# Window attention: heads of a band gathered and projected once per own row, value projection moved ahead

## The chip, the cores and the metric

One Trainium2 chip, one core. The program is one launch; the metric is the device time of the launch in microseconds. TensorE does the matrix products, VectorE and GpSimd elementwise work and small transposes, ScalarE exponentials and copies, SyncE issues the DMA transfers. TensorE's clock has two levels, 1.2 and 2.4 GHz; the profile tells the granted share of the upper one.

## What is computed

The part that the change touches is attention over overlapping windows, cut from the reference (the softmax and the sums are shortened here):

```python
def _L0_conv_ref(x, norm1_w, norm1_b, wq, wk, wv, wproj, ...):      # x (2, 96, 256, 256)
    tops = _positions(h, step, ps); lefts = _positions(w, step, ps)  # ps 16, step 14: 19 x 19 windows
    crop = x[:, :, row_idx[:, None, :, None], col_idx[None, :, None, :]]
    tok = crop.transpose(0, 2, 3, 4, 5, 1).reshape(b * n, ps * ps, c)
    y = _layernorm(tok, norm1_w, norm1_b)
    q, k, v = heads(y @ wq), heads(y @ wk), heads(y @ wv)            # 4 heads, 16 / 16 / 24 wide
    attn = softmax(q k^T / sqrt(16)); out = attn v
    tok = out @ wproj + tok
    acc = zeros_like(x).at[windows].add(tok)
    x2 = acc * fh * fw                  # rows and columns that two windows share count one half each
    ... MLP with a depthwise 5 x 5 convolution on x2, then a clustering block ...
```

Before it, the whole network input is brought to zero mean and unit variance by groups of three channels, which the kernel folds into a scale and a shift for each channel and image (`gn_scale`, `out_shift`, the latter with the projection's constant part).

## The kernel before

The function `attention` walks over 38 bands (19 per image, two images), each a strip of 16 rows by 256 columns, and over the 19 windows of a band, each 16 by 16 = 256 tokens. Band tops and window lefts are 14 apart, the last only 2 after the one before (238, 240). So neighbours share 2 rows or columns, the last two share 14. `own_rows` is the number of rows of a band that no later band touches: 14, for the last but one 2, for the last 16.

All engines run the same loop over windows n = 0 .. 721, written out by hand as a software pipeline. Each engine takes its instructions in the order of the code and waits on counting semaphores. In iteration n TensorE issues:

- `scores_for_max(n, 0)` (line 677): bf16 products of keys and queries for two heads, whose maxima VectorE takes (line 753)
- in windows 5 to 12 of a band, `queries_and_keys` (line 662): one chunk, 512 token columns, of the next band's queries and keys. ScalarE copies it to `packed` (line 613) and SyncE spreads it over the partitions of `q` and `k` in eight transfers for two chunks (line 480)
- `scores(n - 1)` (line 689): 16 records of fp32 products against the queries less maxima (`qaug`, line 777)
- `projection(n - 5)` (line 712): one fp32 product of 256 columns out of `ot`; ScalarE copies it to `prs` (line 632) and GpSimd adds it into `acc` (line 572)
- `scores_for_max(n, 1)`, the other two heads
- `attended(n - 2)` (line 700): the value products, exponentials times values with a column of ones for the denominators
- `values(n - 1)` (line 707): the value projection of a window; ScalarE copies it into `vaug` (line 619)
- `maxima(n)` (line 719): the maxima transposed

VectorE in iteration n: `maxima(n, 0)`, `turn(n - 3)` (line 760, value products to tokens on partitions), `maxima(n, 1)`, `denominators(n - 3)` (line 764), `turn_back(n - 4)` (line 770, a transpose of 256 elements per partition in blocks of 32) and `queries_less_maxima(n)` (line 777). ScalarE: the chunk's copy, `exponential(n - 1, 0)`, `projected(n - 5)`, `exponential(n - 1, 1)` (line 626), `values(n - 1)`. The bank `lin_ps` is shared by the chunk, the projection and the value projection: `lin_free` makes TensorE wait until ScalarE has copied the last one out.

GpSimd: `normalise` (lines 555, 559) multiplies a window by reciprocals and by the half shares; `add`; `turn_columns` (line 542) turns one eighth of the next band's rows to token order, in windows 2 to 9; `scale` (line 549) prepares `acc` as x times scale plus shift; `both` (line 583) adds x once more for the second output. What a band leaves to the next is copied from one `acc` buffer to the other (line 576).

SyncE per band, in this order: load x into `xr` (line 504), spread pair 0, store x2 (line 509), spread pairs 1 and 2, store xs (line 515), load x into `acc` (line 470), spread pair 3, load y (line 466), four transfers that unroll convolution taps (line 490, 768 pieces of 256 bytes each). The x, y and store transfers have one contiguous run of 14336 or 16384 bytes per channel.

## Time and profile before

| | |
|---|---|
| median of three runs | 7228.42 us (7219.73 to 7231.93) |
| span of the profiled execution | 7234.2 us |
| attention stage in it | first window's maxima at 684.7 us, last at 4078.1 us |
| TensorE busy in the whole span | 6229.6 us (86%) |
| VectorE, ScalarE, GpSimd busy | 4977.8, 3555.8, 2561.1 us |

A matrix product is recorded with its drain, so one record overlaps the next and the distance from start to start is what TensorE spends. A fp32 product stands as two records. A timeline row groups instructions of one line that follow each other; what stands in brackets at its end is the idle time of the engine before it and what ended it. The trace's times are microseconds from the start of the span.

### The profile page before, as it was taken

What the parts mean: (1) busy time and instruction counts of PE and PEld (TensorE: products, weight loads), DVE (VectorE), ACT (ScalarE), POOL (GpSimd) and SP (SyncE); (2) the same over time, 40 slices, a digit from 0 to 9 for tenths busy, and PEclk for the clock granted to TensorE, in tenths of its full rate; (3) what the DMA queues carried; (4) which work ended last, traced back from release to release, by engine and by line L of the source; (5) the groups of instructions that cost most, each with busy time, mean ns of one, the idle gap of its engine ahead of it and who ended that gap; (6) DMA issues with size and microseconds to landing.
All of it is one profiled execution on the core that took longest, in us unless ns stands there. A gap on an engine that the chain in (4) does not pass through costs nothing. (4 is left out here: it accounts for less than half of the span.)

```text
span 7234.2 us, 138671 instructions
## 1 busy us (share of the span) xinstructions
PE 6229.6 (86%) x52604; PEld 3161.5 (44%) x52604; DVE 4977.8 (69%) x7538; ACT 3555.8 (49%) x5600; POOL 2561.1 (35%) x3401
## 2 busy tenths in 40 slices
PE   0885999999999999999999689979999566588885
PEld 0332555555554544555555333335555011076662
DVE  6785777777777777777777555548888445556664
ACT  0553666666666666666666356654444111143340
POOL 0443555555555555555555466630000000000000
PEclk9997999999999999999999899999999788789985
DMA  7785454554554444444544378879897999736666
GB/s 304 194 244 152 90 115 113 113 113 112 113 113 92 110 111 112 113 112 114 116 112 103 86 235 237 238 247 355 342 346 279 284 306 311 226 95 191 185 190 180
DMA packets 461711, 1303.16 MB, mean 180 GB/s; under 512 B 158148, under 2 KB 163268, under 8 KB 416964
## 3 DMA queue, kind: packets, MB, share of 16 engines
q1 hardware_dynamic: 400564, 1141.10, 56.2%
q10 hardware_dynamic: 53328, 102.85, 4.8%
q0 software_dynamic: 7168, 50.34, 2.0%
q8 instruction: 432, 7.08, 0.4%
q14 instruction: 219, 1.79, 0.1%
HBM read 731.14 MB, written 508.40 MB: 171 GB/s over the span
## 5 line engine op out<-in xcount | busy, mean ns | idle before, releaser
L753 DVE TENSOR_REDUCE at_mz<-at_ps 128x4 bf16<-128x1024 f32 x1444 | 1774.5, 1229 | 792.1 <-PE at_ps L677 791.5
L626 ACT ACTIVATE at_E<-at_ps 128x1024 f32<-128x1024 f32 x1444 | 1500.7, 1040 | 801.7 <-PE at_ps L689 801.7
L689 PE MATMUL at_ps<-at_qaug,at_k 32*128 32x256 f32 x11552 | 835.2, 403 | 79.2 <-DVE at_qaug L777 78.0
L700 PE MATMUL at_ps<-at_E,at_vaug 128*32 128x256 f32 x11552 | 776.9, 386 | 1.9 <-issue 1.9
L1216 PE MATMUL cv_ps<-cv_yin,cv_band 128*128 128x384 f32 x2304 | 746.0, 486 | 27.5 <-DMA cv_yin<-y_mlp 27.5
L1236 DVE TENSOR_TENSOR cv_yin<-cv_gl,cv_yin 64x384 f32<-64x384 f32 x1152 | 637.5, 553 | 151.3 <-ACT cv_gl L1227 143.5
L689 PEld LDWEIGHTS at_ps<-at_qaug,at_k 32*128 32x128 f32 x11552 | 525.4, 185 | 443.9 <-issue 226.0
L555 POOL TENSOR_TENSOR at_share<-at_rden,t_share 128x8 f32<-128x8 f32 x722 | 146.9, 204 | 1444.7 <-DVE at_rden L764 1444.6
L677 PE MATMUL at_ps<-at_k,at_q 32*128 32x256 bf16 x5776 | 580.7, 277 | 9.5 <-DMA at_k<-at_packed 7.4
L1216 PEld LDWEIGHTS cv_ps<-cv_yin,cv_band 128*128 128x128 f32 x2304 | 436.4, 189 | 337.4 <-DMA cv_yin<-y_mlp 28.4
L1227 ACT ACTIVATE cv_gl<-cv_ps,cv_bias 128x384 f32<-128x384 f32 x576 | 334.4, 581 | 438.4 <-PE cv_ps L1216 438.4
L1498 POOL MEMSET cs_eps<- 96x1 f32 x1 | 0.1, 95 | 1500.9 <-POOLq L1246 1500.9
L707 PEld LDWEIGHTS at_ps<-t_wv,at_y 96*128 96x128 f32 x2888 | 378.0, 190 | 301.2 <-issue 301.2
L707 PE MATMUL at_ps<-t_wv,at_y 96*128 96x96 f32 x2888 | 496.7, 295 | 2.5 <-issue 2.4
L572 POOL TENSOR_TENSOR at_acc<-at_prs,at_acc 96x256 f32<-96x256 f32 x722 | 495.1, 686 | 3.1 <-ACT at_prs L632 3.1
L712 PE MATMUL at_ps<-at_ot,t_wproj_heads 128*96 128x256 f32 x1444 | 487.4, 419 | 2.2 <-ACT at_prs L632 1.8
L559 POOL TENSOR_TENSOR at_on<-at_turned,at_share 128x256 f32<-128x256 f32 x722 | 444.1, 615 | 104.4 <-DVE at_ot L770 1.3
L1754 PE MATMUL cl_ps<-c_rhs,cl_xu 97*128 97x208 f32 x2048 | 445.4, 375 | 40.1 <-DMA cl_xu<-x 33.6
L1364 DVE SCALAR_TENSOR_TENSOR f_xa<-f_ps,f_b,f_xa 128x256 f32<-128x256 f32 x384 | 227.0, 667 | 345.7 <-PE f_ps L1347 344.9
L1754 PEld LDWEIGHTS cl_ps<-c_rhs,cl_xu 97*128 97x128 f32 x2048 | 395.1, 210 | 109.8 <-issue 67.3
L1344 PE MATMUL f_ps<-f_sa,f_wa 128*32 128x512 f32 (+1 forms) x1728 | 236.3, 619 | 239.9 <-DMA f_sbb<-s_mlp 238.3
L632 ACT ACTIVATE at_prs<-at_ps 96x256 f32<-96x256 f32 x722 | 426.9, 591 | 3.9 <-PE at_ps L712 3.6
(210 smaller groups left out, 9384.4 us busy)
## 6 DMA issues: line engine op xcount, KB each, us to landing
cv_yin<-y_mlp SPq DMA_DIRECT2D x48, 2340.0 KB, 14.7
s_mlp<-cv_yin SPq DMA_DIRECT2D x48, 2340.0 KB, 8.3
at_rows_in<-y_attention SPq DMA_DIRECT2D x38, 1536.0 KB, 14.4
gn_xin<-in_x SPq DMA_DIRECT2D x16, 3072.0 KB, 23.2
ln_xin<-in_x SPq DMA_DIRECT2D x192, 256.0 KB, 7.6
y_attention<-ln_xin SPq DMA_DIRECT2D x192, 256.0 KB, 3.8
cl_xu<-x SPq DMA_DIRECT2D x128, 384.0 KB, 3.8
cl_xv<-x SPq DMA_DIRECT2D x64, 768.0 KB, 6.4
```

Source lines behind the costliest of these rows:

```text
L559: pool.tensor_tensor(on[:, s, :].rearrange("p (a d) -> p a d", d=VC), turned[:, s, :].rearrange("p (a d) -> p a d", d=VC), share[:, s, :]. ...
L572: pool.tensor_tensor(a, prs[:, m % 2, :].rearrange("p (r c) -> p r c", c=PS), a, ALU.add).then_inc(added, 1)
L626: act.activation(E[:, m % 2, 2 * p:2 * p + 2, :], psum[:, 2 + 2 * p:4 + 2 * p, :], ACT.Exp).then_inc(exp_done, 1)
L677: i = pe.matmul(psum[:, g, TOK * j:TOK * j + TOK], q_upper[rows, n % 2, tokens(w, 128 * j, 128)], k_upper[rows, n % 2, tokens(w)], start=T ...
L689: i = pe.matmul(psum[:, 2 + h, TOK * j:TOK * j + TOK], k[rows, n % 2, tokens(w, 128 * j, 128)], qaug[rows, m % 2, :], start=True, stop=True)
L700: i = pe.matmul(pv_ps[32 * h:32 * h + VC, 0:TOK], vaug[:, m % 2, z, h, :], E[:, m % 2, h, z * TOK:(z + 1) * TOK], start=(z == 0), stop=(z ...
L707: i = pe.matmul(lin_ps[:, j * C:(j + 1) * C], y[0:C, n % 2, tokens(w, 128 * j, 128)], t["wv"][:], start=True, stop=True)
L712: pe.matmul(lin_ps[0:C, 0:TOK], t["wproj_heads"][:], ot[:, m % 2, :], start=True, stop=True).then_inc(proj_done, 1)
L753: dve.tensor_reduce(mz[:, m % 2].rearrange("p j (h c) -> p h j c", c=32)[:, 2 * p:2 * p + 2, :, DQ], psum[:, 0:2, :].rearrange("p h (j n) ...
L1216: m = pe.matmul(psum[:, n % NB, 0:3 * RUN], band[:, s, c, a, :], yin[:, s, c, 3 * u:3 * u + 3, GAP * a:GAP * a + RUN], start=(a == 0), sto ...
L1236: i = dve.tensor_tensor(yc, gl[half_rows(f), n % NG, :].rearrange("p (t n) -> p t n", n=RUN), yc, ALU.add)
L1754: m = pe.matmul(psum[:, 2 * half + g // 2, 256 * (g % 2):256 * (g % 2) + NFC], xu[:, n % XS, 128 * tile:128 * tile + 128], t["rhs"][:, f * ...
```

## The change

For each window, `normalise` no longer writes a buffer of its own but weighs the turned heads into `heads`, a buffer of 128 column pairs for the whole band. The pair that two windows share is weighted, waited for and added (four GpSimd instructions in place of two). When a group of 16 pairs is complete, after windows 2, 4, 6, 9, 11, 13, 15 and 18 (`WHOLE_AT`), `turn_back` transposes it in one instruction of 512 elements per partition into `ot`, a band buffer with 32 columns x 16 rows per chunk. `save` keeps the rows that the next band shares before they are overwritten, `join` adds them. The projection runs once for each own row, as eight products of 32 columns x own rows (448, 64 or 512 columns), in windows 0 to 7 of the next band; ScalarE copies it with the shift as bias into `xa`, and GpSimd adds x times scale (`residual`, two instructions per chunk, windows 1 to 8) and then x once more (`both`, windows 9 to 16). There is no `acc` and no `prs`, and x is loaded once.

The queries-and-keys chunks move from windows 5 to 12 to windows 8 to 15. `values(n - 1)` stands before `attended(n - 2)` on TensorE, and its copy between the two exponentials on ScalarE. y is loaded, x loaded and xs stored by half rows (128 columns, pieces of 512 bytes); `rows_in` holds half a band and is turned in windows 0 to 3 and 9 to 12. The loop runs eight iterations past the last window in place of five.

The diff, cut to its core:

```diff
+    CC = W // YP
+    PAIRS = W // 2
+    WHOLE_AT = (2, 4, 6, 9, 11, 13, 15, 18)
+    QK_AT = 8
+    END = NW + YP
...
-        rows_in = sb("rows_in", [C, PS * W])
+        rows_in = sb("rows_in", [C, PS, W // 2])
         y = sb("y", [C + 1, 2, W * PS])
-        acc = sb("acc", [C, 2, PS * W])
-        xr = sb("xr", [C, PS * W])
+        heads = sb("heads", [128, PAIRS, VC])
+        ot = sb("ot", [128, W, PS])
+        saved = sb("saved", [128, CC, STEP])
+        xscaled = sb("xscaled", [C, PS, CC])
+        xr = sb("xr", [C, PS, W])
+        xa = sb("xa", [C, PS, W])
...
+        def qk_at(n):
...
+            return (nb + 1, w - QK_AT) if n < NW and nb + 1 < NB and QK_AT <= w < QK_AT + YP else None
+
+        def whole(n):
+
+            nb, w = where(n)
+            return (nb, WHOLE_AT.index(w)) if 0 <= n < NW and w in WHOLE_AT else None
+
+        def proj_at(n):
+
+            nb, w = where(n)
+            return (nb - 1, w) if 1 <= nb <= NB and w < YP else None
...
+            def store_x2(n):
+                rows = own_rows(n)
+                sp.wait_ge(x2_done, YP * (n + 1))
+                sp.dma_start(rows_of(x2, n, 0, rows).rearrange("c r w -> c (r w)"), xa[:, 0:rows, :].rearrange("c r w -> c (r w)")).then_inc(x2_stored, 16)
+
+            def store_xs(n, half):
+                rows = own_rows(n)
+                sp.wait_ge(xs_done, YP * n + YP // 2 * (half + 1))
+                sp.dma_start(half_rows(xs, n, half, rows), xr[:, 0:rows, W // 2 * half:W // 2 * (half + 1)]).then_inc(xs_stored[half], 16)
...
+                more = n + 1 < NB
+                if more:
+                    load_y(n + 1, 1)
+                if n:
+                    store_x2(n - 1)
+                if more:
                     spread_heads(n + 1, 0)
-                if n >= 1:
-                    sp.wait_ge(added, NWIN * n)
-                    sp.dma_start(rows_of(x2, n - 1, 0, rows), acc[:, (n - 1) % 2, 0:rows * W]).then_inc(stored, 16)
-                if n + 1 < NB:
                     spread_heads(n + 1, 1)
+                if n:
+                    store_xs(n - 1, 0)
+                if n + 2 < NB:
+                    load_y(n + 2, 0)
+                if more:
                     spread_heads(n + 1, 2)
-                if n >= 1:
-                    sp.wait_ge(summed, sums(n - 1))
-                    sp.dma_start(rows_of(xs, n - 1, 0, rows), xr[:, 0:rows * W]).then_inc(xs_stored, 16)
-                    sp.wait_ge(stored, 16 * n)
-                    if n + 1 < NB:
-                        if carries(n):
-                            sp.wait_ge(carried, carries(n))
-                        load_x(n + 1)
-                if n + 1 < NB:
+                if n and n < NB:
+                    load_x(n, 0)
+                if more:
                     spread_heads(n + 1, 3)
-                if n + 2 < NB:
-                    load_y(n + 2)
-                if n >= 1:
+                if n:
+                    store_xs(n - 1, 1)
+                    if n < NB:
+                        load_x(n, 1)
                     unroll_taps((n - 1) * PER_BAND, PER_BAND)
...
-                pool.tensor_tensor(on[:, s, :].rearrange("p (a d) -> p a d", d=VC), turned[:, s, :].rearrange("p (a d) -> p a d", d=VC),
-                                   share[:, s, :].unsqueeze(2).to_broadcast([128, 8, VC]), ALU.mult).then_inc(on_done, 1)
-
-            def add(m):
-                n, w = where(m)
-                pool.wait_ge(pr_out, m + 1)
+
+                def shares(a, b):
+                    return share[:, s, a:b].unsqueeze(2).to_broadcast([128, b - a, VC])
+
                 if w == 0:
-                    pool.wait_ge(scaled, pieces(n))
-                    if carries(n):
-                        pool.wait_ge(carried, carries(n))
-                if m:
-                    pool.wait_ge(added, m)
-                a = window(acc, n % 2, w)
-                pool.tensor_tensor(a, prs[:, m % 2, :].rearrange("p (r c) -> p r c", c=PS), a, ALU.add).then_inc(added, 1)
-                if w == NWIN - 1 and n % NWIN < NWIN - 1:
-                    first = STEP if n % NWIN < NWIN - 2 else 2
-                    pool.wait_ge(added, m + 1)
-                    pool.tensor_copy(acc[:, (n + 1) % 2, 0:(PS - first) * W], acc[:, n % 2, first * W:]).then_inc(carried, 1)
-
-            def both(n, piece):
-                if piece == 0:
-                    pool.wait_ge(added, NWIN * (n + 1))
-                    pool.wait_ge(xr_loaded, 16 * (n + 1))
-                rows = slice(piece * 2 * W, (piece + 1) * 2 * W)
-                pool.tensor_tensor(xr[:, rows], xr[:, rows], acc[:, n % 2, rows], ALU.add).then_inc(summed, 1)
+                    pool.tensor_tensor(heads[:, 0:8, :], turned[:, s], shares(0, 8), ALU.mult).then_inc(heads_done, 1)
+                elif w < NWIN - 1:
+                    pool.tensor_scalar(turned[:, s, 0, :], turned[:, s, 0, :], share[:, s, 0:1], None, ALU.mult).then_inc(weighted, 1)
+                    pool.tensor_tensor(heads[:, first + 1:first + 8, :], turned[:, s, 1:8, :], shares(1, 8), ALU.mult)
+                    pool.wait_ge(heads_done, m)
+                    pool.wait_ge(weighted, weightings(m))
+                    pool.tensor_tensor(heads[:, first, :], heads[:, first, :], turned[:, s, 0, :], ALU.add).then_inc(heads_done, 1)
...
+            def save(n, c):
+                rows = shared_rows(n)
+                if rows:
+                    if n % NWIN == 1:
+                        pool.wait_ge(ot_done, YP * (n - 1) + c + 1)
+                    else:
+                        pool.wait_ge(joined, joins(n - 1, c))
+                    if joins(n, c) > 1:
+                        pool.wait_ge(joined, joins(n, c) - 1)
+                    pool.tensor_copy(saved[:, :, 0:rows], ot[:, cols(c), PS - rows:PS]).then_inc(saved_done, 1)
+
+            def join(n, c):
+                rows = shared_rows(n)
+                if rows:
+                    pool.wait_ge(ot_done, YP * n + c + 1)
+                    pool.wait_ge(saved_done, joins(n, c))
+                    a = ot[:, cols(c), 0:rows]
+                    pool.tensor_tensor(a, a, saved[:, :, 0:rows], ALU.add).then_inc(joined, 1)
+
+            def residual(n, c):
+                rows = own_rows(n)
+                if c % 4 == 0:
+                    pool.wait_ge(x_loaded[c // 4], 16 * (n + 1))
+                if YP * n + c:
+                    pool.wait_ge(x2_done, YP * n + c)
+                pool.tensor_scalar(xscaled[:, 0:rows, :], xr[:, 0:rows, cols(c)], t["gn_scale"][:, n // NWIN:n // NWIN + 1], None, ALU.mult).then_inc(scaled, 1)
+                pool.wait_ge(pr_out, YP * n + c + 1)
+                pool.wait_ge(scaled, YP * n + c + 1)
+                a = xa[:, 0:rows, cols(c)]
+                pool.tensor_tensor(a, a, xscaled[:, 0:rows, :], ALU.add).then_inc(x2_done, 1)
+
+            def both(n, c):
...
+            for n in range(END + 1):
+                nb, w = where(n)
+                if whole(n - 5):
+                    join(*whole(n - 5))
                 if 0 <= n - 3 < NW:
                     normalise(n - 3)
-                if n >= 5:
-                    add(n - 5)
-                nb, w = where(n)
-                if nb + 1 < NB and 2 <= w < 2 + YP:
-                    turn_columns(nb + 1, w - 2)
-                if 1 <= nb < NB:
-                    for piece in fresh(nb)[2 * w:2 * w + 2]:
-                        scale(nb, piece)
-                    if 5 <= w < 5 + own_rows(nb - 1) // 2:
-                        both(nb - 1, w - 5)
-            for piece in range(own_rows(NB - 1) // 2):
-                both(NB - 1, piece)
+                if whole(n - 3):
+                    save(*whole(n - 3))
+                if nb + 1 < NB and w < 4:
+                    turn_columns(nb + 1, w)
+                if nb + 1 < NB and 9 <= w < 13:
+                    turn_columns(nb + 1, w - 5)
+                if nb >= 1 and 1 <= w < 1 + YP:
+                    residual(nb - 1, w - 1)
+                if nb >= 1 and nb < NB and 9 <= w < 9 + YP:
+                    both(nb - 1, w - 9)
...
+            def projected(n, c):
+                rows = own_rows(n)
+                act.wait_ge(proj_done, YP * n + c + 1)
+                if c == 0 and n:
+                    act.wait_ge(x2_stored, 16 * n)
+                    act.wait_ge(xs_done, YP * n)
+                act.activation(xa[:, 0:rows, cols(c)].rearrange("p r c -> p c r"), lin_ps[0:C, 0:CC * rows].rearrange("p (c r) -> p c r", r=rows),
+                               ACT.Identity, bias=t["out_shift"][:, n // NWIN:n // NWIN + 1]).then_inc(pr_out, 1)
...
+                if qk_at(n):
+                    queries_and_keys(*qk_at(n))
+                if proj_at(n):
+                    projected(*proj_at(n))
                 if 0 <= n - 1 < NW:
                     exponential(n - 1, 0)
-                if n >= 5:
-                    projected(n - 5)
-                if 0 <= n - 1 < NW:
+                    values(n - 1)
                     exponential(n - 1, 1)
...
+            def projection(n, c):
+                rows = own_rows(n)
+                if shared_rows(n):
+                    pe.wait_ge(joined, joins(n, c))
+                else:
+                    pe.wait_ge(ot_done, YP * n + c + 1)
+                pe.matmul(lin_ps[0:C, 0:CC * rows], t["wproj_heads"][:], ot[:, cols(c), 0:rows], start=True, stop=True).then_inc(proj_done, 1)
...
+            chunks, projected = YP, 0
+            for n in range(END):
                 if n < NW:
                     scores_for_max(n, 0)
-                if chunk_at(n):
-                    lin_free(n - 1, 0, n - 5)
-                    queries_and_keys(*chunk_at(n))
+                if qk_at(n):
+                    lin_free(n - 1, chunks, 0)
+                    queries_and_keys(*qk_at(n))
                     chunks += 1
+                if proj_at(n):
+                    lin_free(min(n - 1, NW), chunks, projected)
+                    projection(*proj_at(n))
+                    projected += 1
                 if 0 <= n - 1 < NW:
                     scores(n - 1)
-                if n >= 5:
-                    lin_free(min(n - 1, NW), chunks, n - 5)
-                    projection(n - 5)
                 if n < NW:
                     scores_for_max(n, 1)
+                if 0 <= n - 1 < NW:
+                    lin_free(n - 1, chunks, projected)
+                    values(n - 1)
                 if 0 <= n - 2 < NW:
                     attended(n - 2)
...
+            def turn_back(n, c):
+                dve.wait_ge(heads_done, NWIN * n + WHOLE_AT[c] + 1)
+                if shared_rows(n):
+                    dve.wait_ge(saved_done, joins(n, c))
+                if n:
+                    dve.wait_ge(proj_done, YP * (n - 1) + c + 1)
+                dve.transpose(ot[:, cols(c), :].rearrange("p c r -> p (c r)"),
+                              heads[:, 16 * c:16 * c + 16, :].rearrange("p a d -> p (a d)")).then_inc(ot_done, 1)
```

## Rows read from the trace of the kernel before

**Rows 1.** Busy time by stretch (busy us and count per engine, PEclk, DMA share, GB/s)
```profile
2500.00:2600.00 100.00, 97.97 (x1040) 50.42 (x1033) 75.58 (x129) 63.23 (x95) 57.73 (x90) 1.00 0.51 113
```

**Rows 2.** Waits in 1500 to 3500 us (total, times, longest us)
```profile
PE at_ps L689 <- DVE at_qaug L777: 44.9, 243, 0.2
```

**Rows 3.** All instructions of line 753 (duration ns min/median/max, first and last start)
```profile
L753 DVE TENSOR_REDUCE at_mz<-at_ps x1444: 1223/1230/1232, 684.7 to 4078.1; 128x4 bf16<-128x1024 f32 x181
```

**Rows 4.** Timeline of TensorE, two windows (start us, us, then the instruction)
```profile
2531.95 0.40 PE L677 MATMUL at_ps<-at_k,at_q 32*128 32x256 bf16 x4
2532.32 1.12 PE L662 MATMUL at_ps<-at_y,t_wqk 97*128 97x512 f32 x2
2533.38 1.15 PE L689 MATMUL at_ps<-at_qaug,at_k 32*128 32x256 f32 x16
...
2537.12 0.40 PE L677 MATMUL at_ps<-at_k,at_q 32*128 32x256 bf16 x4
2537.70 1.15 PE L689 MATMUL at_ps<-at_qaug,at_k 32*128 32x256 f32 x16 [0.18 <-DVE at_qaug L777]
2538.78 0.67 PE L712 MATMUL at_ps<-at_ot,t_wproj_heads 128*96 128x256 f32 x2
2539.39 0.40 PE L677 MATMUL at_ps<-at_k,at_q 32*128 32x256 bf16 x4
2539.72 1.07 PE L700 MATMUL at_ps<-at_E,at_vaug 128*32 128x256 f32 x16
...
2541.24 0.28 PE L719 MATMUL at_ps<-t_neg_eye,at_mz 128*128 128x128 bf16 x2
2541.45 0.40 PE L677 MATMUL at_ps<-at_k,at_q 32*128 32x256 bf16 x4
```

**Rows 5.** Timeline of VectorE in the second of these windows
```profile
2539.83 1.23 DVE L753 TENSOR_REDUCE at_mz<-at_ps 128x4 bf16<-128x1024 f32 x1 [0.69 <-PE at_ps L677]
...
2541.08 0.40 DVE L770 STREAM_TRANSPOSE at_ot<-at_on 128x256 f32<-128x256 f32 x1
2541.55 0.42 DVE L777 TENSOR_TENSOR at_qaug<-at_ps,at_q 128x256 f32<-128x256 f32 x1
```

**Rows 6.** Timeline of ScalarE in both windows
```profile
2533.49 0.60 ACT L613 ACTIVATE at_packed<-at_ps 128x512 f32<-128x512 f32 x1 [1.22 <-PE at_ps L662]
...
2538.92 1.02 ACT L626 ACTIVATE at_E<-at_ps 128x1024 f32<-128x1024 f32 x1 [1.48 <-PE at_ps L689]
2539.84 0.59 ACT L632 ACTIVATE at_prs<-at_ps 96x256 f32<-96x256 f32 x1
2540.22 1.05 ACT L626 ACTIVATE at_E<-at_ps 128x1024 f32<-128x1024 f32 x1
```

**Rows 7.** Groups by line in 1500 to 3500 us, GpSimd (xcount | busy us, mean ns | idle)
```profile
L542 POOL COPY at_y<-at_rows_in 96x512 f32<-96x512 f32 x181 | 192.2, 1062 | 0.0
L583 POOL TENSOR_TENSOR at_xr<-at_xr,at_acc 96x512 f32<-96x512 f32 x151 | 191.3, 1267 | 0.0
...
L549 POOL TENSOR_SCALAR at_acc<-at_acc,t_gn_scale,t_out_shift 96x512 f32<-96x512 f32 x154 | 116.8, 766 | 0.0
```

**Rows 8.** Timeline of SyncE, DMA issues (start us, us until the last is issued)
```profile
2535.46 5.84 SPq L480 DMA_DIRECT2D at_q<-at_packed  x4
2541.35 2.50 SPq L480 DMA_DIRECT2D at_k<-at_packed  x4
...
2544.51 14.25 SPq L490 DMA_DIRECT2D tap_blocks<-tap_lines  x4
```

**Rows 9.** Line 480 in 2541.3 to 2543.8 us, and its landings
```profile
L480 SPq DMA_DIRECT2D at_k<-at_packed x4: 589/594/599, 2541.3 to 2543.3; - x4
...
DMA to landing us min/median/max: 8.8/9.0/10.4
```

**Rows 10.** Timeline of GpSimd at the end of the attention stage
```profile
4091.12 9.79 POOL L583 TENSOR_TENSOR at_xr<-at_xr,at_acc 96x512 f32<-96x512 f32 x8
4108.47 0.10 POOL L987 MEMSET f_eps<- 128x1 f32 x1 [7.56 <-POOLq L378]
```

153 lines of the change are left out of this document (66 added, 87 removed).

## The prediction

> **What bounds the kernel now.** I read the table of stretches first. In 100 us in the middle of the attention stage TensorE is busy 98%, VectorE 76%, ScalarE 63%, GpSimd 58%, and the granted clock is 1.00, the upper of its two levels [rows 1]. In the list of waits TensorE's own products have one entry: the score products wait for VectorE's queries less maxima, 44.9 us in 2000 [rows 2]. So TensorE's order sets the time, and its timeline prices a window. A window in which no queries and keys are projected goes, start to start from 2537.12 [rows 4]: first maxima product 0.58, of which 0.33 is work, as in the second, and 0.25 the wait for VectorE; scores 1.08; projection 0.61; second maxima product 0.33, value products and value projection together 1.52; transposed maxima (L719) 0.21. Sum 4.33 us. A window with a queries-and-keys chunk has 0.37 + 1.06 in place of the 0.58 and takes 5.17 (2531.95 to 2537.12). There are 37 x 8 = 296 of these and 426 of the others: 1530 + 1845 = 3375 us. The maxima run from 684.7 to 4078.1 [rows 3], 721 windows and some 2 us, or 3391 us: the two prices hold to 0.5%.
>
> From the second maxima product to L719 TensorE has 0.33 + 1.52 = 1.85 of work. VectorE needs as much: its reduction starts 0.44 after the product (2539.39 to 2539.83) and takes 1.23 [rows 4, 5], and 0.18 later, at 2541.24, L719 starts, its weight load included. A tie: a shorter TensorE order gains nothing there.
>
> **The change part by part.** Count from the first maxima product of a window as 0.
>
> Projection out of each window. Removed: 722 products of 256 columns, 0.61 each. The clean window keeps its 0.58 up to the scores (the L719, L777, scores path is untouched), then 1.08, so TensorE could start the second maxima product at 1.66. It must wait for the first reduction: 0.44 + 1.23 and some 0.06 for the hand-over, 1.73 (an estimate: the 0.18 above less the load of 128 columns). Then 1.85 and 0.21: **3.80**, 0.53 less than 4.33.
>
> Windows with a chunk. 0.33 + 1.06 + 1.08 + 1.85 + 0.21 = **4.53**, 0.64 less than 5.17; the 0.04 beside the 0.61 is the wait before L662 on the value copy, which now comes between the exponentials.
>
> Projection per own row. 37 bands are projected inside the loop, in the eight windows 0 to 7, which have no chunk. 34 of them have 14 rows, 448 columns. Between 0.61 for 256 and 1.06 for 512 that is 0.61 + 0.75 x 0.45 = 0.95: window 0.33 + 0.95 + 1.08 + 1.85 + 0.21 = **4.42**, 0.09 more than 4.33. One band has 16 rows (4.53, 0.20 more) and two have 2 rows, whose 64 columns fit in the 0.25 wait (3.81, 0.52 less). 130 windows are left clean. The projection adds waits in front of all of TensorE's work: for a chunk's join and for the value copy of the window before. The last chunk of a band is turned back in window 3 of the next, joined in 4 and projected in 7; the value copy is done by 3.8. Free.
>
> Sum: 296 x 0.64 = 189, minus 272 x 0.09 = 24, minus 8 x 0.20 = 2, plus 16 x 0.52 = 8, plus 130 x 0.53 = 69: 240 us.
>
> VectorE's turn back. 722 transposes of 256 elements (0.40, [rows 5]) become 304 of 512. No row has that size; bounds 0.40 and 0.80. I take 0.69, with the slope of the reduction (1.23 for 1024). It stands in front of the queries less maxima, which started 0.07 after the transpose ended (2541.48 to 2541.55), so these come 0.13 later (nothing to 0.35 at the bounds). Where the scores start at 1.39 or 1.28 that is hidden. Two of the eight turns of a band (after windows 15 and 17) are followed by a clean window: 37 x 2 x 0.13 = 10 us, 26 at most.
>
> ScalarE. 722 copies of 0.59 go, 304 of 448 elements come. The old one (L632, 256 elements, stepped write) takes 0.59, the contiguous copy of 512 (L613) 0.60 [rows 6]. Bounds 0.55 and 0.59 x 448/256 = 1.03. L613 starts 1.17 after its product of 512 columns (2532.32 to 2533.49, [rows 4, 6]); this one 1.05 after, at 1.38, and ends by 2.41. The first exponential wants ScalarE at 1.28 + 1.21 = 2.49 (scores to exponential 1.21: 2537.70 to 2538.92 [rows 4, 6]) and the value projection wants the bank at 2.69, so even the upper end is free. The value copy between the exponentials: its product starts at 2.06 in a clean window and is ready some 0.7 later, its four short products done; the first exponential, started at 1.79, frees the engine at 2.71 (0.92 from start to start, [rows 6]). Some 0.05 of wait, and the second exponential (1.05) then ends near 4.1, 0.3 into the next window, whose scores start at 0.58. Free, with 0.3 us of cover; beyond it the scores wait.
>
> GpSimd. Normalise becomes four instructions with some more elements than now, bounded by one scaling (0.77) and by two turning copies (2.12); I take the middle, 1.45. A residual of a chunk is a scaling (0.77 for 512, so 0.69 for 448) and an add (1.27, so 1.13), with some 0.15 between them 1.97; turning a chunk 1.06; adding x once more 1.13 [rows 7]; save or join of 64 elements 0.3. Windows 1 to 3 hold normalise, turn, residual and a save or join, up to 4.8 us in 4.42: a backlog of 1 us. The following windows hold 3.4 to 3.8 and work it off. VectorE's turn back waits for it, with normalise one window before: about 3 us of cover. Nothing on the path. SyncE's store of x2 waits for the last residual, in window 8, and the first spreads stand behind it: issued at 7.4 to 12.4 after window 8 began and landed by 17, before ScalarE wants their buffer in window 12, at 19.6.
>
> SyncE and its queue. x is loaded once, not twice. But loads of y and x and stores of xs now go in halves of a row, 512-byte pieces, 1344 or 1536 to a transfer. The last whole xs store (1536 KB) goes out at 4100.91, where the adds end, and the next stage begins at 4108.47 [rows 10], 7.5 us; a half takes 3.7 to 7.5, I take 5. What is moved is the deadline: the last chunk of queries and keys is copied in window 15, not 12. With window 8 as 0, the copy ends at 33.8 (7 x 4.53 + 2.1) and the next band's first product comes at 8 x 4.53 + 3 x 3.80 = 47.6: 13.8 us for eight transfers. They need 5.0 us to issue (2.50 for four, [rows 8]). Now, behind a store and a load of 1344 KB, four took 5.84 to issue and the last four 8.8 to 10.4 to land [rows 8, 9]: from the copy's end at 2534.1 [rows 6] to the last landing at 2543.3 + 10.4 = 2553.7, 19.6 us. In the changed order the half store goes out at about 25.5 (the add of window 12), then half of y, then eight spreads (5), then at about 33 the half load that stands in front of the last spreads. Their bounds are 5 us with nothing in front and 19.6 with all of today's; with half of the load and no store I take 10 (halfway is 12), landing at 44 to 46. Cost 0, with 2 to 4 us of cover.
>
> [...]
>
> The end. The residual of the last band now comes after its last window. GpSimd then has three normalises (4.5), a save (1), two joins of 448 (2.2), eight residuals of 16 rows (17.6, with 0.77 + 1.27 + wait) and eight adds (10.2), 35.5 us starting some 5 us after the last window began, then a half store of 5: 45. Now it is 33: the last reduction, at 4078.1 [rows 3], starts 0.58 + 1.08 + 0.61 + 0.44 after its window, so that began at 4075.4, and the next stage begins at 4108.47 [rows 10]. Cost 12 us (8 to 18). The start I take as even: half of y is loaded and turned, then the other half, against less traffic before the first spreads (5 either way).
>
> **Sum.** 240 - 10 - 12 = 218 us. The profiled execution spans 7234.2, 0.08% above the median of 7228.4: 7234.2 - 218 = 7016, or 7011 against the median.
>
> **Rivals.**
> (a) The spreads come late. Landing 19.6 us after the copy, as now, would make every band start wait 19.6 - 13.8 = 5.8 us, 37 times 215: 7226. If the half transfers hold SyncE as the small pieces did (14.25 us for 3072 pieces, so 6.2 for 1344 and 7.1 for 1536), store, y load, eight spreads and x load take 6.2 + 7.1 + 5 + 6.2 from 25.5, so the last spreads begin at 50.0 and land at 57.5, 9.9 us late: 366 us, **7377**, slower than before. It decides from 13.8 us; 2 us beyond it cost 74 us (7085). For it: the same queue already shows the 19.6 and the 14.25. Against: the 14.25 came behind 1.5 MB of y and unlanded spreads, and half as much stands in front now.
> (b) ScalarE's stepped write. The new copy writes with a step of 1 KB, the old with 64 bytes. If it took twice the upper bound, 2.06, it would end at 3.44 and hold the value projection 0.75 us in 280 windows: 210 us, 7220. The rows speak against it: the exponential behind the old copy starts 0.38 after it (2539.84 to 2540.22, [rows 6]), so the extra is at its end, not in its rate.
> The Trainium skill (SBUF — State Buffer, Door 1) says that each access that crosses into a new 16-byte line pays a penalty. Both steps do so at every element, so by that rule the new copy costs no more per element than the old one.
> (c) GpSimd behind. If its instructions take 30% more than I price, windows 1 to 3 hold 6.2 us and 4 and 5 some 4.8: 5.4 + 0.8 of backlog when the turn back of window 6 wants its heads, 3 more than the cover: 3 x 37 = 110 us, 7120. With 10% more it is hidden. For it: no row has these short instructions; against: the large ones are priced from their own rows [rows 7].
> (d) More gain. If the 1.85 of the tie was TensorE's and shrinks in the new order, up to 0.05 x 722 = 36: 6975.
>
> **How the numbers follow.** Forecast 0.62 (6975 to 7050, which takes in the bounds of the transpose, the end and the start); (a) 0.19, of which 0.06 ends slower than before and the rest lies between 7050 and 7200; (b) 0.05; (c) 0.08; (d) below 6975 0.04; several small losses that together leave nothing, 0.02. Range **6970 to 7130**: below it 0.03, above it 0.15. A measurement of this kernel tells 0.2% from no change (14 us). Faster 0.87, same 0.04, slower 0.09. Likeliest time 7011.
>
> **What would show it.** Periods of 4.53, 4.42 and 3.80 between first maxima products; in clean windows VectorE idle only before the second reduction, and TensorE waiting for the first one as well as for the queries less maxima. TensorE busy near 96%. No wait of the first maxima product of a band for a transfer into q or k; if there is one, (a). The stepped copy under 1.1 us; if over 1.3, (b). GpSimd with idle time in windows 5 to 18; without, (c). A gap of about 45 us between the last window's start and the next stage. I would be wrong if the tie of 1.85 grew, since each 0.1 there is 72 us.

## The result: 1.7% faster, half of what was forecast

The changed kernel takes 7106.27 us (median of 4 runs, 7094.13 to 7128.61), the kernel before 7226.08 (4 runs, 7219.73 to 7231.93). The ratio is 0.9832, 95% interval 0.9810 to 0.9854: 120 us, or 1.7%, where 215 were forecast. The profiled execution spans 7126.8 us, against 7234.2. It is the slowest of the four, some 20 us above their median, so what is read from its trace lies at the upper end.

The profile after, first by stretch: the middle of the attention stage, and all but its end (busy us and count per engine, then the granted clock of TensorE, DMA share, GB/s).

```profile
2500.00:2600.00 100.00, 98.14 (x1078) 51.92 (x1074) 78.04 (x123) 65.20 (x87) 79.14 (x143) 1.00 0.43 96
685.00:3820.00 3135.00, 3068.36 (x32906) 1616.80 (x32908) 2395.30 (x3740) 1963.60 (x2646) 2302.01 (x4360) 0.97 0.46 97
```

In the 100 us that answer to [rows 1] all is as forecast: TensorE 98%, the clock at its upper level, GpSimd up from 58% to 79%. Over the whole stage the clock is 0.97. Two levels, 1 and 0.5, average to 0.97 when 6% of the time is at the lower one, 1.2 GHz: about 190 us of 3135. The same row of the kernel before has 0.99. (Over the stage up to its last reduction the clock's own records add up to 205 us at the lower level, and 42 in the kernel before.)

Windows of TensorE (start us, us): one with a projection, from 2404.12, and one that is clean, from 2479.53. One with a chunk stands further down, counted from product to product of L720 (2360.70 to 2365.22).

```profile
2404.12 0.40 PE L735 MATMUL at_ps<-at_k,at_q 32*128 32x256 bf16 x4
2404.45 0.99 PE L774 MATMUL at_ps<-at_ot,t_wproj_heads 128*96 128x448 f32 x2
2405.38 1.15 PE L747 MATMUL at_ps<-at_qaug,at_k 32*128 32x256 f32 x16
2406.36 0.39 PE L735 MATMUL at_ps<-at_k,at_q 32*128 32x256 bf16 x4
...
2408.51 0.40 PE L735 MATMUL at_ps<-at_k,at_q 32*128 32x256 bf16 x4
...
2479.53 0.40 PE L735 MATMUL at_ps<-at_k,at_q 32*128 32x256 bf16 x4
2480.11 1.15 PE L747 MATMUL at_ps<-at_qaug,at_k 32*128 32x256 f32 x16 [0.18 <-DVE at_qaug L843]
2481.26 0.40 PE L735 MATMUL at_ps<-at_k,at_q 32*128 32x256 bf16 x4
2481.59 0.69 PE L765 MATMUL at_ps<-t_wv,at_y 96*128 96x96 f32 x4
2482.20 1.07 PE L758 MATMUL at_ps<-at_E,at_vaug 128*32 128x256 f32 x16
2483.21 0.29 PE L781 MATMUL at_ps<-t_neg_eye,at_mz 128*128 128x128 bf16 x2
2483.43 0.40 PE L735 MATMUL at_ps<-at_k,at_q 32*128 32x256 bf16 x4
```

With a chunk, with a projection and clean they take 4.52, 4.39 (2404.12 to 2408.51) and 3.90 us, where 4.53, 4.42 and 3.80 were forecast and the kernel before had 5.17, 4.33 and 4.33 [rows 4]. At these prices a band would take 8 x 4.39 + 8 x 4.52 + 3 x 3.90 = 83.0 us, exactly the forecast 8 x 4.42 + 8 x 4.53 + 3 x 3.80. Yet a band takes 86.4 us in the mean and 84.3 in the median, first reduction to first reduction, and the mean of windows 12, 13, 14 and 15 of a band is 5.89, 5.56, 5.26 and 4.70 us, single ones up to 8.3. These four hold 21.4 - 18.1 = 3.3 us a band too much: 37 x 3.3 = 122 us.

What stands there, in the list of waits of 1500 to 3500 us (total, times, longest), some 23 bands:

```profile
ACT at_packed L670 <- DMA at_k<-at_packed: 71.1, 23, 5.0
PE at_ps L765 <- issue: 29.2, 23, 3.2
```

The first entry is new: in 23 of these 24 bands ScalarE's copy of a chunk waited for transfers that empty its buffer. In the worst of them (SyncE, TensorE and ScalarE by time, then two stretches around it):

```profile
2358.38 0.32 SPq L497 DMA_DIRECT2D x<-at_xa  x1
2358.80 6.92 SPq L512 DMA_DIRECT2D at_q<-at_packed  x4
2360.70 1.12 PE L720 MATMUL at_ps<-at_y,t_wqk 97*128 97x512 f32 x2
2365.22 1.13 PE L720 MATMUL at_ps<-at_y,t_wqk 97*128 97x512 f32 x2
2365.76 2.50 SPq L512 DMA_DIRECT2D at_k<-at_packed  x4
2370.15 0.60 ACT L670 ACTIVATE at_packed<-at_ps 128x512 f32<-128x512 f32 x1 [5.02 <-DMA at_k<-at_packed]
2370.85 0.66 PE L765 MATMUL at_ps<-t_wv,at_y 96*128 96x96 f32 x4 [3.20 <-issue]
```
```profile
2366.00:2371.00 5.00, 1.80 (x22) 1.10 (x22) 2.25 (x4) 0.85 (x2) 4.76 (x10) 1.00 0.61 103
...
2376.00:2382.00 6.00, 6.00 (x47) 3.04 (x43) 2.39 (x5) 2.53 (x4) 2.30 (x5) 0.50 0.96 224
```

The product of the chunk was ready, but the copy (L670) started 4.93 us after it began, not 1.17. The value projection needs the bank that this copy empties and stood still for 3.20 us. TensorE was busy 1.80 of 5 us, and then the granted clock went from 1.00 to 0.50, 2.4 to 1.2 GHz: two windows of 8.3 us. What it waited for is the first eight spreads (L512), which came behind the store of x2 (L497), which came behind the last residual.

Over the whole stage the wait comes in 35 of 36 bands and delays the copy by 0.7 to 2.8 us, by 3.8 in this one. The clock fell after it in 13 of them, for 3.4 to 27.3 us each. The four executions of the changed kernel, 7128.6, 7116.3, 7096.2 and 7094.1 us, had mean granted clocks of 0.928, 0.931, 0.933 and 0.935: the longer, the lower. The band without the wait is the one whose store has 2 rows, 192 KB:

```profile
2268.91 0.32 SPq L497 DMA_DIRECT2D x<-at_xa  x1
2269.34 2.42 SPq L512 DMA_DIRECT2D at_q<-at_packed  x4
```

Its residuals have 64 columns, so the store goes out 6.6 us after window 8 begins and not 9.9, and the four spreads behind it take 2.42 us to issue, not 6 to 7. They land at 14.9.

### The profile page after: what moved, and what is told of

The parts are those of the page before. It is cut to its first block and busy times, and to the rows that moved or that the text cites. A ratio compares the mean times of both kernels' runs of the same rounds, so it can differ in the third digit from the quotient of the medians.

```text
span 7126.8 us, 136670 instructions
## 1 busy us (share of the span) xinstructions
PE 6123.0 (86%) x51768; PEld 3132.6 (44%) x51768; DVE 4906.2 (69%) x7120; ACT 3484.0 (49%) x5182; POOL 3099.7 (43%) x4987
## 5 line engine op out<-in xcount | busy, mean ns | idle before, releaser
L683 ACT ACTIVATE at_E<-at_ps 128x1024 f32<-128x1024 f32 x1444 | 1482.3, 1027 | 414.1 <-PE at_ps L747 395.4
L747 PE MATMUL at_ps<-at_qaug,at_k 32*128 32x256 f32 x11552 | 853.5, 410 | 23.1 <-DVE at_qaug L843 22.9
L758 PE MATMUL at_ps<-at_E,at_vaug 128*32 128x256 f32 x11552 | 791.8, 392 | 0.0
L843 DVE TENSOR_TENSOR at_qaug<-at_ps,at_q 128x256 f32<-128x256 f32 x722 | 303.9, 421 | 284.6 <-PE at_ps L781 284.6
L691 ACT ACTIVATE at_xa<-at_ps,t_out_shift 96x448 f32<-96x448 f32 (+2 forms) x304 | 306.1, 1007 | 342.5 <-PE at_ps L774 342.5
L670 ACT ACTIVATE at_packed<-at_ps 128x512 f32<-128x512 f32 x304 | 181.5, 597 | 549.8 <-PE at_ps L720 432.2
L720 PE MATMUL at_ps<-at_y,t_wqk 97*128 97x512 f32 x608 | 372.0, 696 | 55.9 <-DVE at_k L847 43.5
```

What stands on the lines that cost most here:

```text
L683: act.activation(E[:, m % 2, 2 * p:2 * p + 2, :], psum[:, 2 + 2 * p:4 + 2 * p, :], ACT.Exp).then_inc(exp_done, 1)
L691: act.activation(xa[:, 0:rows, cols(c)].rearrange("p r c -> p c r"), lin_ps[0:C, 0:CC * rows].rearrange("p (c r) -> p c r", r=rows), ACT.I ...
L720: pe.matmul(lin_ps, t["wqk"][:], y[:, n % 2, CK * c:CK * c + CK], start=True, stop=True).then_inc(qk_done, 1)
L747: i = pe.matmul(psum[:, 2 + h, TOK * j:TOK * j + TOK], k[rows, n % 2, tokens(w, 128 * j, 128)], qaug[rows, m % 2, :], start=True, stop=True)
L758: i = pe.matmul(pv_ps[32 * h:32 * h + VC, 0:TOK], vaug[:, m % 2, z, h, :], E[:, m % 2, h, z * TOK:(z + 1) * TOK], start=(z == 0), stop=(z ...
```

## Experiments

**The order of the queue.** One edit to the changed kernel:

```diff
 for n in range(NB + 1):
+    if more:
+        spread_heads(n + 1, 0)
     if n:
         store_x2(n - 1)
     if more:
-        spread_heads(n + 1, 0)
         spread_heads(n + 1, 1)
```

> The changed kernel with one edit: on SyncE the store of x2 stands behind the first eight spreads instead of in front of them. Theory A (the queue order makes ScalarE's copy in window 12 wait, and the lower clock follows from that wait): the first spreads issue about 7 us after window 8 begins and land by 14; the wait of 71 us over 23 bands is gone, windows 12 to 15 all take 4.52 us, time at the lower clock in the attention stage falls from 263 us to about 65 or less, and the time is 7106 - 37 x 3.3 = 6985 us. Theory B (the clock falls by itself, whatever the wait): only the wait itself goes, 37 x 1.35 = 50 us, 7056 us, and windows of 8.3 us are still there. Theory C (the store, now in front of the second eight spreads, delays those instead, and window 14 waits): 7090 to 7106 us.

Measured: 7006.52 us (6999.48 to 7019.66), 0.9684 of the kernel before in the same session (0.9659 to 0.9709), 1.5% less than the changed kernel's 0.9832. SyncE, and the long stretch:

```profile
2385.50 2.42 SPq L512 DMA_DIRECT2D at_q<-at_packed  x4
2387.96 2.49 SPq L512 DMA_DIRECT2D at_k<-at_packed  x4
...
685.00:3820.00 3135.00, 3107.49 (x34242) 1651.01 (x34246) 2491.35 (x3893) 2035.92 (x2749) 2380.05 (x4538) 1.00 0.47 99
```

The eight spreads take 5 us to issue and begin 6.6 us after the first maxima product of window 8; they land at 13.4 (medians of 36 bands). The wait is gone from the list, every median of windows 8 to 15 is 4.52, none is longer than 4.8, and the clock is 1.00. From the first to the last reduction of the stage it takes 3140.3 us, the changed kernel 3270.4: 130 us. Of these TensorE's own standing still is 29.2 / 23 x 37 = 47; the other 83, by subtraction, came from the lower clock that followed: the time at the lower level falls from 205 us to 17, and these 17 are at the stage's start. (The 263 us of the expectation was too high; the trace before the edit has 205.) Theory B is out, since no slow window is left once the wait is; so is C, since the store in front of the second eight does no harm. The time fell by 124 us between the two profiled executions and by some 107 by the ratios. It did not reach the 6985 of theory A, because the 122 us had been read from the changed kernel's slowest execution and then taken off the median: 7128.6 - 122 is 7006.

The Trainium skill (TensorE: Matmul & The Clock Gate, HAM oscillation — how this bites in real kernels) tells of a kernel that waits for DMA between groups of products, falls to the lower clock each time and pays half of the time spent there. The trace agrees on the half: 188 us more at the lower level than in x2_later, of which half is 94, beside the 83 above. It differs on "each time": the clock fell in 13 bands of 35.

**When the store is let go.** The queue left as it is, but no scaling on GpSimd:

```diff
-pool.tensor_scalar(xscaled[:, 0:rows, :], xr[:, 0:rows, cols(c)], t["gn_scale"][:, b], None, ALU.mult).then_inc(scaled, 1)
 pool.wait_ge(pr_out, YP * n + c + 1)
-pool.wait_ge(scaled, YP * n + c + 1)
 a = xa[:, 0:rows, cols(c)]
-pool.tensor_tensor(a, a, xscaled[:, 0:rows, :], ALU.add)
+pool.tensor_tensor(a, a, xr[:, 0:rows, cols(c)], ALU.add)
```

> The changed kernel with GpSimd's multiplication of x by the residual scale left out (the sum is made of the unscaled x, so this part of the computation is missing); the order of the queue on SyncE stays. Theory A1 (the residual comes late because the scaling takes 1.40 us each, and that is what the store of x2 and the spreads behind it wait for): the last residual ends 6 us after window 8 begins instead of 9.9, the spreads land by 17.5, before ScalarE wants their buffer at 19.6, the wait and most of the lower-clock time go, and the end of the stage is some 12 us shorter: 6970 to 6985 us. Theory A2 (what counts is the store itself in front of the spreads, its bytes and its issue, not when it is let go): the wait in window 12 stays, about 7090 us.

Measured: 7005.70 us (6989.52 to 7013.76), 0.9678 (0.9652 to 0.9704). Counted from the first maxima product of window 8, the store goes out at 6.8 us instead of 9.9, the eight spreads land at 18.0 instead of 21.4 (medians of 36 bands), and ScalarE's copy starts at 19.6 without a wait. So the store may stand in front if it is let go early: A1. The time is 20 us above the range of A1, for the same reason as in x2_later: the loop takes 3144.8 us, 126 less than in the profiled execution of the changed kernel, but that one was the slowest of its four.

**One instruction's price.** The changed kernel's scaling has a multiplication alone; the kernel before has a multiplication and an addition in one, at 0.77 us for 512 elements [rows 7]. By the list of groups (xcount | busy us, mean ns), in the changed kernel:

```profile
L629 POOL TENSOR_SCALAR at_xscaled<-at_xr,t_gn_scale 96x448 f32<-96x448 f32 x169 | 236.9, 1402 | 0.0
```

Twice the price taken. Two things differ from the old instruction: its form, and that x is read in short runs. To part them, on the fastest kernel (values_back, below), first the form:

```diff
-pool.tensor_scalar(xscaled[...], xr[:, 0:rows, cols(c)], scale, None, ALU.mult)
+pool.tensor_scalar(xscaled[...], xr[:, 0:rows, cols(c)], scale, shift, ALU.mult, ALU.add)
...
-               ACT.Identity, bias=shift)
+               ACT.Copy)
```

> The kernel values_back with GpSimd's scaling of x written as the kernel before has it, a multiplication and an addition (scale and bias) in one instruction, and ScalarE's copy of the projection without the bias; where it reads x stays as it is, runs of 32 elements 256 apart. If the form with a multiplication alone is what makes it slow, it takes about 0.69 us for 448 elements instead of 1.40, the last residual of a band ends some 5 us earlier, the end of the stage (eight scalings of 1.56 us each in its chain) is 6 us shorter, and the time is 6981 - 6 = 6975 us. If the steps of x are what makes it slow, it takes 1.40 us as before and the time stays at 6981 us.

then the runs:

```diff
-pool.tensor_scalar(xscaled[...], xr[:, 0:rows, cols(c)], scale, None, ALU.mult)
+pool.tensor_scalar(xscaled[...], xr[:, 0:4, W // 2 * (c // 4):W // 2 * (c // 4) + rows * CC // 4], scale, None, ALU.mult)
```

> The kernel values_back with GpSimd's scaling of x reading as many elements in four runs of 112 or 128 instead of 14 or 16 runs of 32 (they are other elements of x, so the residual added is not the window's own); the form with a multiplication alone stays. If the form is what makes it slow, 1.40 us as before, 6981 us. If the short runs are, about 0.7 us and 6975 us.

The line's own rows (duration ns min/median/max), two_ops first:

```profile
L630 POOL TENSOR_SCALAR at_xscaled<-at_xr,t_gn_scale,t_out_shift x20: 705/712/720, 2422.2 to 2599.5; 96x448 f32<-96x448 f32 x20
```
```profile
L630 POOL TENSOR_SCALAR at_xscaled<-at_xr,t_gn_scale x16: 1394/1399/1408, 2436.4 to 2550.6; 96x448 f32<-96x448 f32 x16
```

The form it is: 0.71 with the addition and the same short runs, 1.40 without it and with long ones. The times are 6985.57 us (0.9637, 0.9616 to 0.9659) and 6981.87 (0.9634, 0.9616 to 0.9652), both the same as values_back with 0.9648: with the first spreads in front of the store, nothing in the loop waits for this line. The end of the stage is shorter, though: from the last reduction to the next stage 43.4 us in two_ops and 49.7 in values_back. The expected 6 us are there, and too few to be seen in the whole time.

**That price alone, in the changed kernel.** The same edit of form, with the queue and TensorE's order as the change has them. (It also takes the bias out of ScalarE's copy, which goes from 1.04 to 0.95 us.)

> The changed kernel with the edit of two_ops alone: scaling of x as multiplication and addition in one instruction, ScalarE's copy without the bias. The store of x2 stays in front of the first spreads, and the value projection stays in front of the value products. If the step of the prediction that failed is the price of this one instruction (0.69 us taken, 1.40 measured, eight of them ahead of the store), the last residual now ends about 4 to 7 us after window 8 begins instead of 9.9, the spreads land some 3 to 6 us earlier, by 17.5 of the 19.6 us that ScalarE leaves them, the wait in window 12 and the stretches at the lower clock go, and the time is 7106 - 122 - 6 = 6980 us, up to 7010. If the cover was too short even at the predicted price (the issue of eight spreads takes 8 us, not 5), a part of the wait stays: 7040 to 7090 us.

Measured: 7003.81 us (6995.99 to 7013.28), 0.9674 (0.9652 to 0.9696). SyncE in one band, and the entry of the list of waits, 1500 to 3500 us:

```profile
2391.07 0.32 SPq L497 DMA_DIRECT2D x<-at_xa  x1
2391.49 5.99 SPq L512 DMA_DIRECT2D at_q<-at_packed  x4
2397.52 3.18 SPq L512 DMA_DIRECT2D at_k<-at_packed  x4
```
```profile
ACT at_packed L670 <- DMA at_k<-at_packed: 1.5, 1, 1.5
```

The wait is down from 71.1 us to 1.5. By the medians, counted as above (in the band shown from 2383.40), the store goes out at 7.7, the spreads begin at 8.1 and land at 19.0, and ScalarE wants the buffer at 19.6: 0.6 us of cover. The eight spreads behind the store take 8.9 us to issue (here 2391.49 to 2400.70, 9.2) and 5.0 without it (x2_later). So with the queue as it is this one instruction's price decides, and the rest of the cover was eaten by the issue.

**The value projection's place.** x2_later with the old order:

```diff
 # TensorE
+attended(n - 2)
 lin_free(n - 1, chunks, projected)
 values(n - 1)
-attended(n - 2)
 # ScalarE
 exponential(n - 1, 0)
-values(n - 1)
 exponential(n - 1, 1)
+values(n - 1)
```

> The kernel x2_later with the value projection put back where the kernel before has it, behind the value products on TensorE, and its copy back behind the second exponential on ScalarE. By the prediction's reading the move is worth 0.04 us in each of eight chunk windows of 37 bands: 12 us slower than x2_later, 6997 us. Rival (the move costs 0.10 us in each window, since the hand-over ahead of the value products takes 0.61 us in the changed kernel and 0.52 in the one before): 20 to 60 us faster than x2_later, 6925 to 6965 us.

Measured: 6981.26 us (6978.98 to 6984.13), 0.9648 (0.9625 to 0.9670): 25 us less than x2_later by the medians, within the rival's 20 to 60. The intervals of the two ratios overlap, but the ranges of the times don't, and from the first to the last reduction it takes 3118.3 us, 22 less. That part of the change costs more than it gains. Two windows of values_back: one with a chunk, from the second maxima product on, then a clean one with a row of VectorE ahead of it.

```profile
2392.19 0.39 PE L736 MATMUL at_ps<-at_k,at_q 32*128 32x256 bf16 x4
2392.51 1.07 PE L759 MATMUL at_ps<-at_E,at_vaug 128*32 128x256 f32 x16
2393.52 0.69 PE L766 MATMUL at_ps<-t_wv,at_y 96*128 96x96 f32 x4
2394.04 0.28 PE L782 MATMUL at_ps<-t_neg_eye,at_mz 128*128 128x128 bf16 x2
...
2408.76 0.44 DVE L824 STREAM_TRANSPOSE at_turned<-at_ps 128x256 f32<-128x256 f32 x1
2408.91 0.40 PE L736 MATMUL at_ps<-at_k,at_q 32*128 32x256 bf16 x4
2409.35 1.07 PE L759 MATMUL at_ps<-at_E,at_vaug 128*32 128x256 f32 x16
2410.35 0.69 PE L766 MATMUL at_ps<-t_wv,at_y 96*128 96x96 f32 x4
2410.87 0.28 PE L782 MATMUL at_ps<-t_neg_eye,at_mz 128*128 128x128 bf16 x2
```

The first needs 0.32 + 1.01 + 0.52 = 1.85 us from the second maxima product to the transposed maxima, as the kernel before does [rows 4]. The changed kernel needs 0.33 + 0.61 + 1.01 = 1.95 (2481.26 to 2483.21). The value projection takes 0.61 where the value products follow it and 0.52 where the transposed maxima do. By the medians it is 1.94 in x2_later and 1.84 in values_back in all 592 windows with a chunk or a projection, so the 0.10 us of the rival is there. The new order gives a part of it back: the product of the chunk or of the projection starts 0.33 us after the first maxima product, and 0.39 in the old order. Counted at TensorE the windows take 4.52 and 4.39 us in x2_later, 4.48 and 4.35 in values_back; 16 x 0.04 x 37 = 24 us, and 22 are measured. The prediction's reading had the gain and not the cost, the rival the cost and not the gain.

The clean windows take 3.90 us in either order. In the old one the value products start 0.44 us after the maxima product and not 0.33, 0.15 after VectorE's turn (L824) has ended, which they wait for (`turned_done`): 0.44 + 1.00 + 0.52 = 1.96.

**The same move in the kernel before.** TensorE's value projection in front of the value products, ScalarE's copy of it between the exponentials, nothing else:

> The kernel before with that part of the change alone: the value projection in front of the value products, its copy between the copy of the projection and the second exponential. By the prediction's reading the chunk windows go from 5.17 to 5.13 us and nothing else moves: 7226 - 12 = 7214 us. Rival (the new order costs 0.10 us of hand-over in each of 16 windows of 37 bands): 7226 + 59 = 7286 us.

Measured: 7882.69 us (7868.06 to 7903.79), 1.0886 (1.0854 to 1.0918). Neither 7214 nor 7286: both expectations had forgotten the bank. A clean window (all engines by time, cut):

```profile
2831.04 0.67 PE L712 MATMUL at_ps<-at_ot,t_wproj_heads 128*96 128x256 f32 x2
2831.18 1.02 ACT L626 ACTIVATE at_E<-at_ps 128x1024 f32<-128x1024 f32 x1 [1.67 <-PE at_ps L689]
2831.65 0.40 PE L677 MATMUL at_ps<-at_k,at_q 32*128 32x256 bf16 x4
2832.10 0.58 ACT L632 ACTIVATE at_prs<-at_ps 96x256 f32<-96x256 f32 x1
2832.83 0.66 PE L707 MATMUL at_ps<-t_wv,at_y 96*128 96x96 f32 x4 [0.78 <-ACT at_prs L632]
```

Projection and value projection write the same bank. The projection is put behind the scores, its copy (L632) behind the first exponential, and in the old order the value products, 1.0 us long, hid that copy. Moved in front of them, the value projection starts 1.18 us after the second maxima product (2831.65 to 2832.83), where 0.33 would do, and the window takes 5.25 us. To see whether it is the copy:

```diff
 # ScalarE, on before_values_moved
-if 0 <= n - 1 < NW:
-    exponential(n - 1, 0)
 if n >= 5:
     projected(n - 5)
 if 0 <= n - 1 < NW:
+    exponential(n - 1, 0)
     values(n - 1)
     exponential(n - 1, 1)
```

> The kernel before_values_moved with one edit: on ScalarE the copy of the projection stands in front of the first exponential instead of behind it. Theory (the value projection needs the bank of partial sums that this copy empties, and the copy stood behind the first exponential of 1.02 us, so that TensorE idled 0.78 us in each window for it and VectorE then for the rest): the copy is done before the scores are, the wait of the value projection for the copy of the projection goes, and clean windows take 4.3 to 4.5 us, the time is 7200 to 7350 us. Rival (the value products behind the value projection and its copy are what cost, whatever the copy of the projection does): windows stay at 5.25 us and the time stays at about 7880 us.

Measured: 7630.08 us (two runs, 7627.80 and 7632.36), 1.0531 (1.0507 to 1.0556). In between, and outside both expectations: clean windows of 4.92 us.

```profile
2768.25 0.67 PE L711 MATMUL at_ps<-at_ot,t_wproj_heads 128*96 128x256 f32 x2
2768.96 0.59 ACT L632 ACTIVATE at_prs<-at_ps 96x256 f32<-96x256 f32 x1 [2.24 <-PE at_ps L711]
2768.86 0.40 PE L676 MATMUL at_ps<-at_k,at_q 32*128 32x256 bf16 x4
2769.70 0.66 PE L706 MATMUL at_ps<-t_wv,at_y 96*128 96x96 f32 x4 [0.44 <-ACT at_prs L632]
```

The exponential accounts for a third of a microsecond (5.25 to 4.92); the rest is the path itself. The projection issues at 2768.25, its copy can't start before 2768.96 and ends at 2769.55, and the value projection would have been due at 2769.19, 0.33 after the second maxima product. The theory named the right resource and was wrong on its size. The changed kernel's projection stands in front of the scores, a whole microsecond earlier, and its list of waits has no such entry; that this place is what spares it is argued from the order, no run moves it alone. The change's two parts are not independent: the second one alone makes the old kernel 9% slower.

## Why the forecast was half right

The sum was 240 us for the windows, less 10 and 12, from the profiled 7234.2. The measured 7106 lies within the stated 6970 to 7130, but outside the 6975 to 7050 that the forecast's own chance was given to. It is there by luck: what took half of the gain is a wait that the prediction had put at nothing, and not one of the small losses or late last spreads that the upper part of the range was meant for.

**Windows: right.** 4.39, 4.52 and 3.90 for 4.42, 4.53 and 3.80. The 0.10 of the clean window is the growth of the "tie of 1.85" to 1.95, named beforehand as the way to be wrong. It costs little because in chunk windows a gain offsets it: the second maxima product follows the scores by 0.98, not 1.08, with no projection between. The growth comes from the order of value projection and value products, 1.94 in every kind of window against 1.84 in values_back; there clean windows keep 1.96, by VectorE's turn. Why the value projection takes 0.61 in one place and 0.52 in the other stays open.

Undisturbed, in x2_later, the loop takes 3140 us, 253 less than before, where 240 - 10 was forecast. At the measured prices the windows give 237 of it. Some 16 more are not in any price: ten windows of the kernel before, of those numbered 15 to 18, took up to 8.8 us in the profiled execution. What held them was not followed up.

**VectorE's turn back: right in size, free in effect.** 0.66 us for 512 elements (0.69 taken); the 10 us charged for it did not come, since the queries less maxima start 0.11 us after the first maxima product with it (2483.54) or without. **ScalarE's stepped copy: free**, though at its upper bound: 1.04 us (bounds 0.55 and 1.03), idle in front of it. Rival (b) is out by its time. The argument against it (the extra is at the copy's end, not in its rate) was wrong: 64, 448 and 512 elements take 0.37, 1.04 and 1.15 us, 1.7 ns for each further element, and at 448 elements 2.3 ns each, as in the old copy of 256 in 0.59. **The last spreads, rival (a) as written: not seen.** The list of waits of the changed kernel from 700 to 3800 us has no entry of the first maxima product for a transfer, and the half transfers took 0.3 us to issue in the median and 2.0 at most, where (a) needed 6.2 to 7.1. But it was nearer than forecast: in x2_later and form_alone the last spreads land 1.1 us before the next band's first product in the median of 36 bands, 0.1 in the closest, where 2 to 4 us were given. **Rival (c), GpSimd behind: its engine, not its path.** GpSimd's price was short by 0.7 us a residual, but VectorE's turn back hardly waits for the heads (0.6 us in 2000); the store of x2 waits for the residuals. **Rival (d): not seen**, the 1.85 grew.

**The cover of the first spreads: the step that failed.** It was one sentence at the end of the paragraph on GpSimd: the store of x2 waits for the last residual, the spreads are "issued at 7.4 to 12.4 after window 8 began and landed by 17, before ScalarE wants their buffer in window 12, at 19.6". Medians measured in the changed kernel: issue from 10.4, landing at 21.4, the buffer wanted at 19.6. Two terms in it were too small. The scaling is the first: 0.69 us taken from the row of a two-part instruction, 1.40 measured; eight of them are 5.7 us more of GpSimd time ahead of the store, 2.3 of which come out as delay. With 0.71 (form_alone) the issue starts at 8.1. The issue is the second: 5.0 us taken, 8.9 behind a store of 1.4 MB, so the landing is 19.0 even then, not 17; a third term, 4.6 us from the last issue to its landing where 2.0 to 2.3 are measured, was too large and hid a part. The second error alone leaves hardly a wait, as form_alone shows (1.5 us in 2000). The first alone would too, by the medians (10.4 + 5.0 + 2.3 = 17.7), but no run has it by itself; together they made the wait. The timeline of the kernel before had a sign of the second: four spreads behind a store took 5.84 us [rows 8]. It was used for the last spreads, and not for the first.

And the consequence was priced nowhere. A wait of TensorE of 1.3 us a band is 47 us; with the lower clock behind it, 130 in the profiled execution. Rival (a) charged its late transfers at their length alone.

**The end: 12 forecast, 20 measured, the same cause.** From the last reduction to the next stage it takes 30.3 us before and 50.1 in the changed kernel. The end of the changed kernel on GpSimd:

```profile
3988.62 1.56 POOL L629 TENSOR_SCALAR at_xscaled<-at_xr,t_gn_scale 96x512 f32<-96x512 f32 x1
...
3991.54 9.72 POOL L639 TENSOR_TENSOR at_xr<-at_xr,at_xa 96x512 f32<-96x512 f32 x8
4006.36 0.10 POOL L1053 MEMSET f_eps<- 128x1 f32 x1 [5.10 <-POOLq L383]
```

Eight scalings at 1.56 instead of 0.77 are 6.3 us; with the other form (form_alone) it is 43.7, 13.4 more than before. The half store takes the 5 us it was given.

Once that instruction costs what it was thought to cost, the change brings 230 us (form_alone, 7003.81 against 7234.32 of the kernel before measured beside it), where 218 were forecast. The surplus is mostly the 10 us that the turn back did not cost and the 16 us of slow windows before, so the sum came out closer than its terms. The gap between the forecast and 7106 is one line's price, on a queue where the issue was underpriced as well, and the clock.

## What to carry to other kernels

A deadline held by a few microseconds of cover deserves the same care as the terms of the sum: write down each step ahead of it on its engine and in its queue, price each at its worst neighbour row, and charge a miss with the lower clock that can follow when TensorE stands still (here in 13 of 35 bands, and for more time than the wait itself). In a queue served in order, put a transfer that someone waits for in front of one that waits for the slowest engine, if nobody wants the latter soon. And take parts of a change singly: here one part gave the gain, the other cost 22 us, and 9% in the kernel before, where a copy from the shared bank lay in between; the fastest kernels are values_back and two_ops, at 0.9648 and 0.9637 of the time before.

## What the runs showed of the hardware

On GpSimd a multiplication of 96 x 448 elements by a value per partition takes 1.40 us and the same with an addition behind it, in one instruction, 0.71; runs of 32 or of 112 elements make no difference. The instruction that does more is twice as fast. The difference is in the rate: 64, 448 and 512 elements take 0.44, 1.40 and 1.56 us with the multiplication alone, 2.5 ns for each further element, and 0.39, 0.71 and 0.77 with both, 0.84 ns (after and two_ops). The Trainium skill (GPSIMD Engine Reference, Elementwise — side-by-side cycle accounting) gives 768 ns as the best case for 512 elements. The row of the kernel before, 766 ns [rows 7], agrees, and the 1.56 us of the multiplication alone is twice that.

Eight spreads of 64 KB took 5.0 us to issue on SyncE with nothing in front of them and 8.5 to 9.7 right behind a store of 1.4 MB; most of the difference is in the first four (2.42 against 6 to 7 us). Right behind a store of 192 KB the first four took 2.42 again.

In the changed kernel TensorE's granted clock went from 1.00 to 0.50 after the engine had stood still for 3.20 us (2367 to 2371) and fell after 13 of 35 such waits in the stage, most of them shorter. The time at the lower level, 205 us against 17 without the waits, comes with 83 us of the 130 that the stage is longer.
